# A vision tower layer on one core: how x is loaded and summed, which engine splits the stacks, where the mask is added, and in which order each engine works

## The chip, the cores and the metric

The kernel runs on one core of one Trainium2 chip. The metric is the device time of one execution in microseconds, as the median of several runs. Engines: TensorE (PE; its weight loads are PEld), VectorE (DVE), ScalarE (ACT), GpSimd (POOL), SyncE (SP, which here only issues DMAs).

## The reference, cut to what matters

```python
# x: (64, 12, 224, 224) f32
pooled = x.reshape(64, 12, 14, 16, 14, 16).sum(axis=(3, 5))        # sums of 16x16 patches
h = einsum('bcij,ce->bije', pooled, channel_weights)               # (64, 196, 192)
n = layernorm(h)
# attention of 12 heads with causal mask (-10000 above the diagonal), and
selection = softmax((n @ sel_w + sel_b) / temperature)[..., 1:]
_, idx = top_k(selection[..., 0], 14)          # 14 of 196 tokens of an image
h = h + (n with attn_output * selection added at the rows idx)
out = h + gelu(layernorm(h) @ in_weight.T + in_bias) @ out_weight  # hidden 768
```

Each token of h is a combination of 12 channel sums, so most of the work is done on 12 or 13 numbers for each token. Attention is computed for the 14 chosen tokens of each image alone.

## The kernel before, in words

The 64 images are 16 groups (g) of 4. For a group:

- **L, the patch sums.** x of a group comes in 7 tiles of 128 partitions x 2688 numbers (3 x 4 image rows of 224). `load_x` (L300) puts the first two of each four rows into a ring of 7 buffers, from SyncE's queue; when they have landed, GpSimd issues an accumulating DMA for the other two rows (`add_halves`, L339). `sum_tile` (L855) then reduces 1344 numbers to 42 on VectorE. After the seventh tile SyncE stores R to a scratch tensor (L307), waits for it and loads it back in another layout (Praw, L315). GpSimd adds the four quarters (L348 to L355).
- **A, the tokens.** `tm` (L444) multiplies by the moments; VectorE computes variance and the first reciprocal root (`var`), `zt` transposes z, `fm` copies it to FM. `log`, `e`, `sel` give the selection, `sl`, `top`, `st`, `slots` the 14 chosen tokens (MAX8 and MATCH_REPLACE8, L936 to L954, then one-hot Sg).
- **K, the stacks.** VectorE computes the second reciprocal root (`var2`), v26, and two differences; ScalarE splits them into bf16 parts (H, M, L, L642); TensorE transposes (L472) and ScalarE copies to Stk1 and Stk2 (L648, L653).
- **f and O, the dense FFN.** 12 matmuls `f` (L555) into one PSUM bank, each followed by a Gelu on ScalarE (L692) before the next may start. 7 output tiles `O` of 6 f32 matmuls (two passes each: 12 instructions, L567) and one bf16 (L571). Tile i takes the tokens i, i + 7, i + 14, ..., so its stationary operand is read with a step of 7 numbers (`tile_of`).
- **G and S, attention of the chosen tokens.** `ga`, `u` (L483 to L496), `sc` the scores (L506), the mask added and the maximum taken on VectorE (L1008, L1012), exponentials on ScalarE (L665), scaled by the reciprocal sum (L670), transposed (`et`, L512), copied (`t`, L674), `g` (L518), `at` (L527).
- **C, the FFN of the chosen tokens**, for two groups together: `xh` (VectorE, L1036 to L1044), `xt`, `fa`, `fb` (L542), `f2` (L547), `os` (L1051), and an indirect store from GpSimd (L362).

Every engine runs a `plan` by itself, a list of `stage:step:lag`; in period k it does the step for group k - lag. What comes first in the list is done first, and waits hold up all that is behind them. TensorE's and VectorE's lists before:

```
PE:  A:tm:1 S:sc:2 O:3:2 A:zt:1 O:4:2 O:5:2 S:et:2 K:tr1:1 S:g:2 K:tr2:1 f:0:1 o:6.0:2 f:1:1 ... f:6:1 o:6.6:2 A:sl:1
     f:7:1 at:0:2 ... f:11:1 O:0:1 A:st:1 O:1:1 G:ga:1 C:xt:2 C:fa:2 G:u:1 O:2:1 C:fb:2 C:f2:2
DVE: L:0 A:var:1 S:sc:2 A:log:1 L:1 A:var2:1 K:v:1 S:ri:2 L:2 K:d1:1 A:sel:1 L:3 K:d2:1 S:g:2 A:top:1
     L:4 S:at:2 A:slots:1 C:xh:2 L:5 G:ga:1 L:6 G:u:1 C:os:2
```

Before the periods, the weights are folded; the copies of these results from PSUM are VectorE's (`weights_heads`, `weights_attention`, `weights_ffn`, in `prepare`), between the first sums.

Of the kernel before, what the change touches and what calls it, by code (L numbers as in the profile page):

```python
# [6 lines left out]
N = IMG // PATCH  # L7
# [3 lines left out]
GB = 4  # L11
# [20 lines left out]
ODD = 64  # L32
PROWS = ODD + SLOTS
# [11 lines left out]
NX = 7  # L45
AHEAD = 2
END = NG + 3
# [60 lines left out]
def program(nc, x, cw, wqkv, bqkv, selw, selb, ow, ob, temp, w1t, b1, w2, consts, e48, e13r, out):  # L108
# [9 lines left out]
    with ExitStack() as ctx:  # L118
# [11 lines left out]
        def kc(name, rows=128):  # L130
# [20 lines left out]
        X = sb("X", [128, NX, TQ * QB // 2])  # L151
# [4 lines left out]
        FM = [sb(f"FM{i}", [ZR, T]) for i in range(2)]  # L156
        prod = sb("prod", [HALF, 2, BC])

        sc = {n: sb(n, [HALF, 2 * GB]) for n in ("var", "lr", "L", "t1", "t2", "s2", "al", "den", "rden")}
# [7 lines left out]
        Sg = sb("Sg", [HALF, 2, 2, SLOTS])  # L167
# [8 lines left out]
        RM = sb("RM", [ROWS, T])  # L176
        UB = sb("UB", [ZR, HP, 2, SLOTS])
# [28 lines left out]
        w_cw, w_ffn, w_att = sem("channel_weights_loaded"), sem("ffn_weights_loaded"), sem("attention_weights_loaded")  # L206
        x_in = [sem(f"x_loaded{k}") for k in range(NX)]
        x_added = [sem(f"x_halves_added{k}") for k in range(NX)]
# [23 lines left out]
        dve_S = Steps(sem("dve_attention"), "sm mx nm ri g0 g1 h1")  # L232
# [13 lines left out]
        dve_W = Steps(sem("dve_weights"), "wr0 ws0 xh0 h10 as0 ini idb ms ms2 wcs rf mr mr2 wcr bw0 bw1 wt ws cf cf2 raw sd sd2 s1 tp tz tmm tmd tmb m1 "  # L246
                      + " ".join(f"{n}{t}" for t in "MR" for n in splits.split()) + " q k v a4 b2 ob")
# [44 lines left out]

        def tile_of(ap, i):

            return ap.rearrange("p (m i) -> p i m", i=FT)[:, i, :]

        @block.sync
        def _(sp):
            def load_x(i, c):
                sp.dma_start(buffer_of(c), half_rows(i, c, 0)).then_inc(x_in[c % NX], 16)  # L300

            def after_tile(i, c):

                if c % XT == XT - 1:
                    g, r = 4 * i + c // XT, (c // XT) % 2
                    sp.wait_ge(dve_L, 4 * XT * i + c + 1)
                    sp.dma_start(scratch[bass.ds(g, 1)].rearrange("o p q -> (o p) q"), R[:, r, :]).then_inc(sums_out[r], 16)  # L307
                if not isinstance(i, int) or c + NX < NT:
                    sp.wait_ge(dve_L, 4 * XT * i + c + 1)
                    load_x(i, c + NX)  # L310
                if c % XT == XT - 1:
                    sp.wait_ge(sums_out[r], landed(g, r))
                    if exists(g - 2):
                        sp.wait_ge(pool_P.sem, pool_P.at(g - 2, "q23"))
                    sp.dma_start(Praw[:, r, :], sums_in[bass.ds(g, 1)].rearrange("o p q -> (o p) q")).then_inc(sums_back[r], 16)  # L315

            for c in range(NX):
                load_x(0, c)
            for c in range(AHEAD):
                after_tile(0, c)  # L320

            def body(i, k):
                for s in range(XT):
                    c = XT * k + s + AHEAD
                    if not isinstance(i, int) or c < NT:
                        after_tile(i, c)

            periods(nc.sync, body, 3, 2)
            for r in range(2):
                sp.wait_ge(sums_out[r], landed(NG - 2 + r, r))  # L330
                sp.wait_ge(y_out[r], landed(NG - 2 + r, r))
                sp.wait_ge(scat[r], landed(NG - 2 + r, r))

        @block.gpsimd
        def _(pool):
            def add_halves(i, c):
                pool.wait_ge(x_in[c % NX], use_of(i, c))
                by_itself(pool)
                pool.dma_start(buffer_of(c), half_rows(i, c, 1), accum_op=ALU.add).then_inc(x_added[c % NX], 16)  # L339
# [17 lines left out]
            def store_chosen(g, k, e, q):  # L357
# [4 lines left out]
                pool.indirect_dma_start(orows, bass.IndirectOffsetOnAxis(ap=idx[k % 4][:, 0:1], axis=0), OS[e][:, :], None  # L362
                                        ).then_inc(scat[e], 16)

            def body(i, k):
                for s in range(XT):
                    c = XT * k + s + AHEAD
                    if not isinstance(i, int) or c < NT:
                        add_halves(i, c)
                    if s == 1 and k % 2 == 0:  # L370
                        for e in range(2):
                            g = 4 * i + k - 4 + e
                            if active(g):
                                store_chosen(g, k + e, e, 2 * i + k // 2 - 2)
# [757 lines left out]
```

## Time and profile before

| | us |
|---|---|
| median of 3 runs (range) | 1082.65 (1079.1 to 1088.77) |
| the profiled execution | 1094.46 |
| its span, first to last instruction | 1092.3 |

The profile is of one execution. Its span is cut into engine busy times, waits and a chain of work that ended last. "Granted clock" is the share of full speed (2.4 GHz) that TensorE was given; it has the levels 1.2 and 2.4 GHz, and a mean between them is a mixture in time. A matmul's mean duration contains its latency; how densely a run of them follows is told by the timeline, which merges them.

### The profile page before, as it was taken

The numbers are of one execution on the slowest core, as the hardware profiler recorded it, in microseconds if no ns is written. First come the engines' busy times: TensorE is split into PE (matmuls) and PEld (weight loads), VectorE is DVE, ScalarE is ACT, GpSimd is POOL, SyncE is SP. The second block draws the span as 40 slices with busy tenths as digits, with TensorE's granted clock in tenths as the row PEclk, the third lists the DMA queues.
The fourth block names the chain that finished last, engine by engine and source line by source line (L and its number), as shares of the span: only waits on it lengthen the run. The fifth ranks groups of instructions, "written<-read, shape, count | busy, mean of one in ns | idle before, by whom it ended". The sixth has DMA issues, their size and how long they took to land.

```text
span 1092.3 us, 12505 instructions
## 1 busy us (share of the span) xinstructions
PE 797.3 (73%) x3860; PEld 624.2 (57%) x3860; DVE 489.6 (45%) x1468; ACT 349.2 (32%) x826; POOL 188.4 (17%) x180
## 2 busy tenths in 40 slices
PE   0632868686868868686877868686887969787885
PEld 0420747466565746466564846466573847567564
DVE  2653545446362535446272544546263454534111
ACT  0003152524333151524334151523325152424331
POOL 2130303013030403013030303013030222000000
PEclk9955669688887869688777879788676877788876
DMA  9999696958595687948595686958595594410000
GB/s 288 265 218 238 145 220 158 229 127 187 144 233 146 148 185 174 213 122 190 139 228 152 147 192 166 222 127 182 141 218 134 141 227 106 80 34 4 23 1 25
DMA packets 97864, 172.52 MB, mean 158 GB/s; under 512 B 5224, under 2 KB 94504, under 8 KB 97802
## 3 DMA queue, kind: packets, MB, share of 16 engines
q0 software_dynamic: 45312, 77.77, 40.4%
q1 hardware_dynamic: 48128, 81.90, 23.4%
q10 hardware_dynamic: 4362, 12.07, 3.4%
q8 instruction: 34, 0.56, 0.2%
q14 instruction: 28, 0.23, 0.1%
HBM read 158.99 MB, written 12.73 MB: 157 GB/s over the span
## 4 chain that ended last, share of the span: by engine, by line
PE 42%; DVE 19%; issue 13%; DMA 12%; ACT 12%; POOL 1%; ACTq 0%; POOLq 0%; DVEq 0%; SPq 0%
PE psO L567 13%; DMA X<-in_x 10%; PE psS L518 6%; PE psF L555 5%; ACT act L692 4%; DVE R L855 3%; PE psC L542 3%; PE psS L512 3%; ACT Sm L670 3%; PE psA L472 2%; PE psS L491 2%; PE psC L547 2%; ACT L692 2%; PE psS L527 2%; DVE mx L1012 2%
## 5 line engine op out<-in xcount | busy, mean ns | idle before, releaser
L567 PE MATMUL psO<-W,act 128*112 128x192 f32 x1344 | 362.8, 421 | 9.4 <-ACT act L692 9.4
L567 PEld LDWEIGHTS psO<-W,act 128*112 128x112 f32 x1344 | 319.3, 299 | 29.5 <-ACT act L692 13.5
L855 DVE TENSOR_REDUCE R<-X 128x42 f32<-128x1344 f32 x112 | 172.4, 1540 | 76.6 <-DMA X<-in_x 76.3
L339 POOL DMA_DIRECT2D X<-in_x x112 | 146.8, 2214 | 75.4 <-DMA X<-in_x 68.7
L692 ACT ACTIVATE act<-psF 128x392 f32<-128x392 f32 x192 | 95.4, 497 | 94.9 <-PE psF L555 94.7
L699 ACT ACTIVATE obuf<-psO 112x192 f32<-112x192 f32 x112 | 36.4, 325 | 276.9 <-PE psO L571 276.8
L555 PE MATMUL psF<-Stk,M1S 104*128 104x392 bf16 x192 | 79.6, 415 | 56.2 <-ACT act L692 55.6
L348 POOL TENSOR_TENSOR Pt<-Praw 48x196 f32<-48x196 f32 x16 | 8.6, 538 | 623.0 <-DMA Praw<-patch_sums 623.0
L512 PE MATMUL psS<-K,Sm 112*98 112x112 f32 x192 | 37.9, 383 | 74.4 <-ACT Sm L670 74.4
L555 PEld LDWEIGHTS psF<-Stk,M1S 104*128 104x128 bf16 x192 | 19.6, 102 | 120.4 <-ACT act L692 120.4
L1022 DVE TENSOR_TENSOR G<-psS,K 64x336 f32<-64x336 f32 x32 | 16.0, 500 | 142.6 <-PE psS L518 142.1
L512 PEld LDWEIGHTS psS<-K,Sm 112*98 112x98 f32 x192 | 32.2, 193 | 77.0 <-ACT Sm L670 77.0
L518 PE MATMUL psS<-ET,F 98*64 98x336 f32 x128 | 73.9, 758 | 1.5 <-ACT ET L674 1.5
L936 DVE MAX8 m8a<-psA 4x8 f32<-4x196 f32 x16 | 5.7, 358 | 140.6 <-PE psA L455 140.6
L472 PE MATMUL psA<-identb,SP 98*104 98x98 bf16 x256 | 27.3, 275 | 45.9 <-ACT SP L642 45.0
L472 PEld LDWEIGHTS psA<-identb,SP 98*104 98x104 bf16 x256 | 22.4, 184 | 65.2 <-issue 41.9
L362 POOL DMA_INDIRECT out<-OS,idx x16 | 15.4, 960 | 200.4 <-DVE OS L1051 197.9
L518 PEld LDWEIGHTS psS<-ET,F 98*64 98x64 f32 x128 | 26.7, 224 | 34.9 <-issue 31.7
L665 ACT ACTIVATE Sm<-Sm,nm 112x196 f32<-112x196 f32 x96 | 42.7, 446 | 8.4 <-DVE nm L1014 8.4
L542 PE MATMUL psC<-XH,W1T 97*128 97x112 f32 x192 | 37.7, 372 | 4.2 <-ACT XH L680 3.5
L527 PE MATMUL psS<-B,G 128*56 128x192 f32 x192 | 40.7, 337 | 0.0
L542 PEld LDWEIGHTS psC<-XH,W1T 97*128 97x128 f32 x192 | 34.9, 278 | 6.7 <-ACT XH L680 5.6
(190 smaller groups left out, 961.3 us busy)
## 6 DMA issues: line engine op xcount, KB each, us to landing
X<-in_x SPq DMA_DIRECT2D x112, 672.0 KB, 10.2
X<-in_x POOLq DMA_DIRECT2D x112, 672.0 KB, 16.5
out<-obuf ACTq DMA_DIRECT2D x16, 588.0 KB, 3.6
patch_sums<-R SPq DMA_DIRECT2D x16, 147.0 KB, 2.6
Praw<-patch_sums SPq DMA_DIRECT2D x16, 147.0 KB, 3.3
W1T<-in_w1t ACTq DMA_DIRECT2D x1, 576.0 KB
W<-in_w ACTq DMA_DIRECT2D x1, 576.0 KB
K<-in_consts ACTq DMA_DIRECT2D x1, 452.5 KB
```

What stands on the lines that cost most here:

```text
L339: pool.dma_start(buffer_of(c), half_rows(i, c, 1), accum_op=ALU.add).then_inc(x_added[c % NX], 16)
L472: mm = pe.transpose(to[0:SK, c0:c0 + HALF], SP[:, 2 * n + k, :, :].rearrange("p n c -> p (n c)"), identb[0:HALF, 0:HALF])
L512: mm = pe.transpose(psS[0:HALF, n // 4, (n % 4) * ROWS:(n % 4 + 1) * ROWS], Sm[:, j, k * HALF:(k + 1) * HALF], kc("ident")[0:ROWS, 0:ROWS])
L518: mm = pe.matmul(psS[0:ZR, 1 + i, 0:3 * ROWS], F[r][:, k, 0:ZR], ET[:, k * HP + 3 * i:k * HP + 3 * i + 3, :].rearrange("p j s -> p (j s)") ...
L527: mm = pe.matmul(psS[0:SLOTS, 0, 0:D], G2[:, j, :], B2[:, j, :], start=(j == 0), stop=(j == HP - 1))
L542: mm = pe.matmul(psC[:, (h % HA) * ROWS:(h % HA + 1) * ROWS], W1T[bias_first(k), k, h * 128:(h + 1) * 128], XH[bias_first(k), k, :], start ...
L555: pe.matmul(psF[:, 0:GT // 2], M1S[:, (n // 2) * 128:(n // 2 + 1) * 128], Stk1[u % 2][:, (n % 2) * (GT // 2):(n % 2 + 1) * (GT // 2)], sta ...
L567: pe.matmul(to, tile_of(act_sb[u % 2][:, m, :], i), W2[:, m, :], start=(m == 0), stop=False)
L665: act.activation(Sm[:, j, :], Sm[:, j, :], ACT.Exp, bias=nm[:, j:j + 1], accum_out=rsum[:, j:j + 1]).then_inc(act_S.sem, 1)
L692: act.activation(act_sb[u % 2][:, n // 2, (n % 2) * (GT // 2):(n % 2 + 1) * (GT // 2)], psF[:, 0:GT // 2], ACT.Gelu).then_inc(act_F1.sem, 1)
L699: act.activation(obuf[u % 2][:, i, :], psO[(i + u) % 2][0:OT, 0:D], ACT.Copy).then_inc(act_F2.sem, 1)
L855: dve.tensor_reduce(R[:, r, t * TQ * N:(t + 1) * TQ * N].rearrange("p (q j) -> p q j", q=TQ), v[:, :, :, :, :], AX.XY, ALU.add).then_inc(d ...
```

## The change

It does the following:

- x comes by plain loads of whole tiles, one buffer for each of the 7 tiles; no accumulating DMA is left (`ADDED` is empty). Tiles 1, 2, 4 and 6 are summed whole by VectorE (2688 numbers); for tiles 0, 3 and 5 GpSimd first adds the second half of the rows to the first (`halve`), and VectorE sums 1344.
- The second reciprocal root, v26 and both differences move from VectorE to GpSimd.
- Stk1 and Stk2 are written in tile order, by a strided read of PSUM, so that the stationary operands of O are contiguous.
- R's store and reload are issued by ScalarE (`R:st`, `R:ld`); SyncE only loads x.
- The mask is 56 more rows of the score matmul's operands (FM's rows 64 to 119 hold 0 or 1, UB's hold -10000 on a diagonal); the instruction that added it is gone, and the exponentials read PSUM.
- ScalarE takes the copies of the folded weights; the large weight loads wait for tiles 1, 3 and 6 of x. The first group's start is written out by hand.
- All four lists are new, O goes in three pieces, and VectorE and GpSimd count their periods one and two later.

```diff
-NX = 7
-AHEAD = 2
-END = NG + 3
+ADDED = ()
+HALVED = (0, 3, 5)
+END = NG + 5
-        X = sb("X", [128, NX, TQ * QB // 2])
+        X = [sb(f"X{k}", [128, TQ * QB // (2 if k in ADDED else 1)]) for k in range(XT)]
...
             def body(i, k):                                     # sync
+                g = 4 * i + k - 1
+                for t in range(XT):
+                    if active(g + 1):
+                        if exists(g):
+                            sp.wait_ge(dve_L, XT * g + t + 1)
...
+                            sp.dma_start(X[t][:, :], tile_in(g + 1, t).rearrange("o p q -> (o p) q")).then_inc(x_in[t], 16)
...
+            def halve(g, t):                                    # gpsimd
+                pool.wait_ge(x_in[t], loaded(g))
+                v = X[t][:, :].rearrange("p (q r w) -> p q r w", q=TQ, r=QR)
+                pool.tensor_tensor(v[:, :, 0:2, :], v[:, :, 0:2, :], v[:, :, 2:4, :], ALU.add).then_inc(x_halved[t], 1)
...
+            def second_variance(g):
+                pool.wait_ge(dve_R1.sem, dve_R1.at(g, "y2"))
...
+                rsqrt(g, pool_R2, n2)
...
+                    pool.tensor_tensor(d1[:, :, :], v26[:, :, :], SP[:, :, 0, :], ALU.subtract).then_inc(pool_K.sem, 1)
...
+            plan = ("H:3:1 P:s:2 H:5:1 c:s:5 A:var2:2 K:v:2 K:d1:2 K:d2:2 H:0:0").split()
...
-                    pe.matmul(to, tile_of(act_sb[u % 2][:, m, :], i), W2[:, m, :], start=(m == 0), stop=False)
+                    pe.matmul(to, act_sb[u % 2][:, m, i * OT:(i + 1) * OT], W2[:, m, :], start=(m == 0), stop=False)
...
+            plan = ("o:1.2:2 o:2.0:2 o:2.1:2 S:et:2 o:2.2:2 o:3.0:2 o:3.1:2 o:3.2:2 S:g:2 K:tr1:1 o:4.0:2 o:4.1:2 "
+                    "K:tr2:1 f:0:1 at:0:2 A:sl:1 at:1:2 at:2:2 f:1:1 o:4.2:2 f:2:1 o:5.0:2 f:3:1 A:st:1 o:5.1:2 "
+                    "f:4:1 G:ga:1 f:5:1 o:5.2:2 f:6:1 G:u:1 f:7:1 o:6.0:2 C:xt:2 o:6.1:2 C:fa:2 f:8:1 o:6.2:2 f:9:1 "
+                    "S:sc:1 f:10:1 C:fb:2 f:11:1 A:tm:0 C:f2:2 o:0.0:1 o:0.1:1 o:0.2:1 o:1.0:1 A:zt:0 o:1.1:1").split()
...
-                    act.activation(Stk1[u % 2][:, :], psA[:, :].bitcast(bf16)[0:SK, 0:GT], ACT.Copy).then_inc(act_K.sem, 1)
+                    act.activation(by_tile(Stk1[u % 2]), tokens_by_tile(psA[:, :].bitcast(bf16)[0:SK, 0:GT]), ACT.Copy).then_inc(act_K.sem, 1)
...
-                    act.activation(Sm[:, j, :], Sm[:, j, :], ACT.Exp, bias=nm[:, j:j + 1],
+                    act.activation(Sm[:, j, :], psS[0:ROWS, j // 2, (j % 2) * T:(j % 2 + 1) * T], ACT.Exp, bias=nm[:, j:j + 1],
...
+            plan = ("S:e2:2 S:e3:2 S:e4:2 S:e5:2 O:0:2 S:n:2 A:fm:1 O:1:2 A:e:1 S:t:2 K:H:1 K:M:1 O:2:2 K:L:1 O:3:2 "
+                    "R:st:0 K:k1:1 K:k2:1 f:0:1 f:1:1 f:2:1 f:3:1 f:4:1 R:ld:0 f:5:1 O:4:2 f:6:1 f:7:1 C:XH:2 O:5:2 "
+                    "G:rs:1 f:8:1 C:ga:2 O:6:2 f:9:1 f:10:1 C:gb:2 f:11:1 S:e0:1 S:e1:1").split()
...
-                    dve.tensor_tensor(Sm[:, :, :].rearrange("p (k j) t -> p k j t", k=3),
-                                      psS[0:ROWS, :, 0:2 * T].rearrange("p k (j t) -> p k j t", j=2),
-                                      RM[:, :].unsqueeze(1).unsqueeze(1).broadcast_to([ROWS, 3, 2, T]), ALU.add).then_inc(dve_S.sem, 1)
...
+            plan = ("A:sel:2 S:g:3 L:0:0 A:top:2 S:at:3 A:slots:2 G:ga:2 C:xh:3 L:1:0 G:u:2 L:2:0 S:sc:2 A:var:1 "
+                    "L:3:0 S:ri:2 A:log:1 L:4:0 C:os:3 L:5:0 L:6:0").split()
```

## Rows read from the trace of the kernel before

**Rows 1.** The profile page: the span and its instructions

```profile
span 1092.3 us, 12505 instructions
```

**Rows 2.** Two windows: length, busy us by engine, granted clock, DMA share, GB/s

```profile
0.00:60.00 60.00, 18.28 (x164) 14.13 (x164) 29.06 (x70) 1.28 (x1) 11.96 (x13) 1.00 1.05 275
503.30:626.30 123.00, 95.73 (x456) 75.15 (x456) 58.13 (x176) 43.41 (x103) 23.31 (x24) 0.79 0.74 172
```

**Rows 3.** One line's instructions, f: ns min/median/max, first and last start

```profile
L555 PE MATMUL psF<-Stk,M1S x192: 331/340/527, 100.5 to 1029.3; 104*128 104x392 bf16 x192
```

**Rows 4.** The chain that ended last, in order of time, 540 to 630 us

```profile
539.23 2.55 DMA patch_sums<-R
...
547.37 8.21 DMA X<-in_x
```

**Rows 5.** Waits, whole run: total us, times, longest us

```profile
DVE R L855 <- DMA X<-in_x: 76.3, 19, 17.3
```

**Rows 6.** Timeline: start, us, twelve f32 matmul instructions of 192 columns

```profile
555.85 4.20 PE L567 MATMUL psO<-W,act 128*112 128x192 f32 x12
...
618.22 2.21 PE L547 MATMUL psC<-W,actS 128*120 128x192 f32 x12 [0.45 <-ACT actS L686]
...
622.89 2.75 PE L567 MATMUL psO<-W,act 128*112 128x192 f32 x12
```

**Rows 7.** Weight loads by line: ns min/median/max, first and last start

```profile
L567 PEld LDWEIGHTS psO<-W,act x1344: 275/300/311, 115.5 to 1067.3; 128*112 128x112 f32 x192
...
L506 PEld LDWEIGHTS psS<-FM,UB x192: 169/173/308, 132.1 to 1045.0; 64*112 64x112 f32 x192
```

**Rows 8.** Groups of VectorE: busy us, mean ns of one

```profile
L855 DVE TENSOR_REDUCE R<-X 128x42 f32<-128x1344 f32 x112 | 172.4, 1540 | 76.6 <-DMA X<-in_x 76.3
...
L1008 DVE TENSOR_TENSOR Sm<-psS,RM 112x1176 f32<-112x1176 f32 x16 | 22.0, 1377 | 5.8 <-PE psS L506 5.8
```

**Rows 9.** GpSimd's elementwise work: a group, and one memset with its ns

```profile
L348 POOL TENSOR_TENSOR Pt<-Praw 48x196 f32<-48x196 f32 x16 | 8.6, 538 | 623.0 <-DMA Praw<-patch_sums 623.0
...
L1127 POOL MEMSET const-float32-0.0<- x1: 99/99/99, 0.4 to 0.4; 128x1 f32 x1
```

**Rows 10.** SyncE's DMA queue: packets, MB, share of 16 engines over the span

```profile
q1 hardware_dynamic: 48128, 81.90, 23.4%
```

**Rows 11.** Timeline, choosing tokens: first and last of eight VectorE instructions

```profile
534.26 0.36 DVE L936 MAX8 m8a<-psA 4x8 f32<-4x196 f32 x1 [8.81 <-PE psA L455]
...
537.26 0.35 DVE L954 TENSOR_TENSOR srow<-cum,mask 4x196 f32<-4x196 f32 x1
```

**Rows 12.** Timeline, queries and scores: ga, UB's two copies, and a score block

```profile
545.41 0.52 PE L483 MATMUL psS<-Sg,F 98*112 98x56 f32 x4
...
548.47 0.90 DVE L1001 TENSOR_TENSOR UB<-psS,K 64x336 f32<-64x336 f32 x2
...
620.81 2.16 PE L506 MATMUL psS<-FM,UB 64*112 64x196 f32 x12
```

**Rows 13.** Timeline, softmax at the end of the run: table load to ET's copies

```profile
1048.69 1.28 ACT L665 ACT_TABLE_LOAD   x1
...
1058.35 1.41 ACT L674 ACTIVATE ET<-psS 98x448 f32<-98x448 f32 x3 [2.35 <-PE psS L512]
```

**Rows 14.** Groups of ScalarE in the stacks: busy us, mean ns of one

```profile
L653 ACT ACTIVATE Stk<-psA 104x784 bf16<-104x784 bf16 x16 | 13.2, 823 | 67.1 <-PE psA L472 67.1
...
L642 ACT ACTIVATE SP<-v 98x624 bf16<-98x624 f32 x16 | 11.7, 730 | 27.4 <-DVE v L975 27.4
```

**Rows 15.** Timeline, chosen tokens normalised: first and last VectorE instruction of xh

```profile
600.57 0.35 DVE L1036 BATCH_NORM_STATS2 bst<-h 120x6 f32<-120x192 f32 x1
...
604.43 0.38 DVE L1044 TENSOR_SCALAR xh<-h,mv,y_lnC 120x192 f32<-120x192 f32 x1
```

**Rows 16.** Timeline, first variance: F's copy, and its last product

```profile
557.07 0.37 DVE L895 COPY F<-psA 98x216 f32<-98x216 f32 x1
...
560.61 0.26 DVE L904 TENSOR_TENSOR F<-F,y_ln 98x96 f32<-98x96 f32 x1
```

More of the change, by code:

```diff
@@ L32 @@
 ODD = 64
+KM = ZR + SLOTS
 PROWS = ODD + SLOTS
@@ L317, in _ @@
[L317 to L320, printed above, removed]
-            def body(i, k):
[L323 to L328, printed above, removed]
+            def body(i, k):
+                g = 4 * i + k - 1
[3 more added lines that the diff above has]
+                            sp.wait_ge(dve_L, XT * g + t + 1)
+                        if t in ADDED:
+                            sp.dma_start(half_tile(t), half_rows(g + 1, t, 0)).then_inc(x_in[t], 16)
+                        else:
+                            sp.dma_start(X[t][:, :], tile_in(g + 1, t).rearrange("o p q -> (o p) q")).then_inc(x_in[t], 16)
@@ L329, in _ @@
+            periods(nc.sync, body, 3, 3)
             for r in range(2):
@@ new lines, in _ @@
+            plan = ("H:3:1 P:s:2 H:5:1 c:s:5 A:var2:2 K:v:2 K:d1:2 K:d2:2 H:0:0").split()
+            def body(i, k):
+                for what in plan:
+                    stage, step, lag = what.split(":")
+                    g, u = 4 * i + k - int(lag), (k - int(lag)) % 4
+                    if not active(g):
+                        continue
+                    if stage == "X":
+                        add_halves(g, int(step))
+                    elif stage == "H":
+                        halve(g, int(step))
+                    elif stage == "P":
+                        sum_quarters(g, u % 2)
+                    elif stage == "K":
+                        stage_K(g, u, step)
+                    elif stage == "A":
+                        second_variance(g)
+                    elif u % 2:
+                        for e in range(2):
+                            store_chosen(g - 1 + e, u - 1 + e, e, pair_of(i, k, lag))
@@ L383, in _ @@
+            periods(nc.gpsimd, body, 5, 2)
         @block.tensor
@@ L712, in body @@
                     g, u = 4 * i + k - int(lag), (k - int(lag)) % 4
-                    if not active(g):
+                    if not active(g) or (stage == "R" and isinstance(g, int) and g == 0):
                         continue
                     if stage == "C":
-                        if k % 2:
-                            step_C(2 * i + k // 2 - 1, step)
+                        if u % 2:
+                            step_C(pair_of(i, k, lag), step)
                     elif stage == "O":
@@ L722, in body @@
                     else:
[L723 removed]
+                        {"A": step_A, "G": step_G, "K": step_K, "R": step_R, "S": step_S}[stage](g, u, step)
             weights()
[L726 removed]
+            weights_heads()
+            step_R(0, 0, "st")
+            step_R(0, 0, "ld")
+            weights_attention()
+            periods(nc.scalar, body, 6, 2)
         @block.vector
```

418 lines of the change are left out of this document (219 added, 199 removed).

## The prediction

> **What bounds the kernel now.** Read first the page's span [rows 1] and the windows [rows 2]. Two groups (one without and one with the FFN of the chosen tokens, C) take 123.0 us, or 61.5 each. No engine fills that: TensorE is busy 95.73 us of it at a mean granted clock of 0.79, VectorE 58.13, ScalarE 43.41, GpSimd 23.31, and DMA 0.74. So it is a ring of steps that hand over to each other, while the in-order lists leave each engine idle at its own hand-over. The first matmul f starts at 100.5 us and the last at 1029.3 [rows 3]; that is 928.8 us for 15 periods and one set of twelve f's, and 63.0 us of the span lie behind it.
>
> Second, the chain in order of time [rows 4]: from the store of the sums at 539.23 to GpSimd's next x DMA at 547.37 are 8.1 us, for store, reload and three quarter sums; then 8.21 us of waiting for x. GpSimd issues the accumulating half of x behind the quarter sums, SyncE issues loads behind the store. VectorE's wait for x totals 76.3 us [rows 5]. Third, the timeline: twelve matmul instructions of 192 columns take 2.75 us for an O tile, 2.21 us for `f2`, and 4.20 us for an O tile when the clock is low [rows 6]. At the high clock O is thus held back by something `f2` does not have, its stationary operand with a step of 7: such a load is 300 ns in the median, a contiguous one of the same 112 columns 173 [rows 7].
>
> **Part by part, for one group.**
>
> *O in tile order.* Seven tiles at 2.75 - 2.21 = 0.54 us less are 3.8 us, and the bf16 loads a little more: 4.2. At the low clock the columns themselves bind (4.20 us is more than either), and nothing is gained. Bounds 0 to 4.6; I take 4.2, as TensorE will seldom be idle for long. The price is a strided read by ScalarE's two stack copies, 0.82 us each [rows 14]. No strided read of PSUM is timed there; I bound it from nothing to as much again, 1.6 us a group, and take 0.5.
>
> *Sums.* VectorE's 1344 numbers take 1.54 us [rows 8]. The mask's addition, 1176 numbers with the same kind of fixed part, takes 1.38, so a number costs about 1 ns and a whole tile 1.54 + 1.40 = 2.94. Four whole and three halved tiles are 16.4 us against 10.8: 5.6 more. VectorE loses the mask's 1.38 and the moved root, v26 and differences, some 25 small instructions, about 4.2 us together (an estimate at 0.17 us each). It stays at 29 us of a group [rows 2], below any period in question, but its 3-us pieces now stand in the ring.
>
> *GpSimd.* 196 numbers take 0.538 us and a memset of one number 0.099 [rows 9]; the difference gives 2.24 ns a number, hence 3.1 us for `halve` (1344), from 1.5 (if it ran as VectorE) to 3.7 (if all scaled): 9.3 us for three. The second root is 18 instructions of 8 numbers, one waiting for the other. Bounds 0.10 and 0.54 us each plus a hand-over near 0.1; I take 0.25, the row nearest in size being the memset: 4.5 us. v26 is 0.8 and a difference 0.56. All with the quarter sums 18 us a group, against 61.5 available.
>
> The Trainium skill's GPSIMD Engine Reference, section Elementwise, gives 4497 ns for a tensor_tensor of 2048 numbers, in proportion 2.95 us for `halve`: 0.5 us a group less, which changes nothing here.
>
> *x.* Plain loads moved 81.90 MB in 23.4% of the span [rows 10], 255.6 us, thus 320 GB/s; 9.6 MB a group and 0.9 of output and sums are 33 us. Every buffer is refilled a period ahead. With no transfer behind GpSimd's list, the 8.21 us of [rows 4] are hidden by the period of lead; if a period fell to 33 us they would return. The store and reload sit in ScalarE's list before the stack copies and after the fourth Gelu. `R:st` waits for the last sum, and K:k1, both stack copies and all Gelus are queued behind it; I cost it at 0.4 us of issue and up to 1 us of wait.
>
> *The new ring, without C.* First from f to f: choosing the tokens is 537.61 - 534.26 = 3.35 us [rows 11], after an estimated 2.5 us of transposes and the sum L:0; then, estimated from like instructions, 0.6 for `st`, 1.0 for h1 and the one-hot. From ga to the end of UB's copies are 549.37 - 545.41 = 4.0 [rows 12], and the sum L:1 is put between them, 2.94. Scores 2.16, the last two f's 1.3. Total 17.9. Then from the last f to the next first: matmul 0.34 [rows 3] and Gelu, estimated from its size beside [rows 14], 0.50; from the table load to the end of ET's copies 1059.76 - 1048.69 = 11.1 [rows 13], plus 0.9 because L:3 (1.54) stands before `ri`; the stacks 2 x 0.73 + 0.57 and two differences, with hand-overs 3.5 [rows 9, 14]; two transposes and the first copy with `R:st` 2.5. Total 18.8. The other branch, tm 1.1 (an estimate: four small matmuls behind the last f), variance 3.8 [rows 16], root 4.5 and v26 0.8, arrives after 10.2, when the first part has used 11.9: covered, by 1.7 us and the transposes. Period 36.7. With C, the normalisation on VectorE is 604.81 - 600.57 = 4.2 [rows 15] and fb 1.1: 42.0. Mean 39.4. TensorE's own work is 95.73 x 0.79 / 2 = 37.8 us a group at the high clock [rows 2], less 4.2 for O: 34 us, now spread between these steps, so it has little slack: some of the steps at the low clock, hand-overs and collisions in the lists I estimate at 10%, 3.6 us. I take 43 us, with 39 and 50 as ends.
>
> *Start.* Group 0's x and the weights are 11.4 MB, at the 275 GB/s of the first 60 us [rows 2] 41.5 us; last sum 2.9; VectorE's weight splits and two sums of group 1, 13; variance 3.8; root and v26 5.5; stacks 3.5, transposes and copy 2. First f at 72 instead of 100.5; bounds 62 and 85. *End.* The old table load of the last scores stands at 1048.69, 19.4 us behind the last f [rows 3, 13]; in the new list it follows after 0.84, so 63.0 - 18.6 = 44.4; with the other steps 43. Twelve f's of the last group without sums between them 15.
>
> *Sum.* 72 + 15 x 43 + 15 + 43 = 775, and 2 us around the span (1094.46 against 1092.3) 777. The median stands at 1082.65 / 1094.46 = 0.989 of the profiled execution: **769 us**.
>
> **The rivals.**
>
> *GpSimd's small instructions are dear.* At 0.54 + 0.18 each the root takes 13 us, not 4.5, and the 1.7 us of cover are gone: with the transposes as only cover, 7 more a period. A period of 50: 72 + 750 + 58 + 2 = 882, times 0.989: 872. For it: [rows 9] have no dependent small instruction. Against: the memset.
>
> *GpSimd and VectorE block each other.* Where a `halve` holds up a VectorE instruction of the variance or the selection, it costs up to 3.1 us each; half of the three in the ring is 4.7 us a period, 47.7, and by the same sum 838 us. In [rows 16] the steps follow undisturbed, but there GpSimd does nothing of this kind.
>
> The Trainium skill's SBUF — State Buffer, section Who interferes with whom, says that a VectorE instruction with two SBUF inputs and a GpSimd instruction that reads SBUF exclude each other for the whole instruction. By that rule this rival is real; no row of before has the pair at the same time.
>
> *The clock stays at 0.79* [rows 2]. 34 us at the high level become 43 on TensorE alone, and with 4 of unhidden latency 47: 828 us.
>
> *Only the x waits and O go; the ring is not otherwise loosened.* 61.5 less 4.1, less 4.2: 53, and 917 us.
>
> *Slower.* The place is GpSimd's list: the differences d1, d2 and then `halve` 0, for which VectorE's L:0 waits, with the choosing of tokens and all of the next f's behind. This loop decides once a period is over 64 us: it has to grow by 21 us and the 1.7 of cover, so its 21 chained instructions would have to take 1.3 us each instead of 0.25. Then the time is 1095 or more (a period of 65). Against: [rows 9] end at 0.54.
>
> **How the numbers follow.** Forecast 0.58, dear small instructions 0.15, low clock 0.10, blocking 0.08, only x and O 0.07, slower 0.02. The likeliest case has its own range of 715 to 825 (periods of 40 to 46). To leave out no more than 2 in 10 it must take in most of the first rival: 705 to 880. A measurement of this kernel tells about 1% from no change. Faster by over 1%: 0.96, within 1% 0.01, slower 0.03.
>
> **What would show it.** O tiles of twelve instructions at 2.2 us; whole sums at 2.9 us and `halve` at 3.1; no wait for x over 1 us after the start; the first f near 72 us; granted clock over 0.85; GpSimd's root near 4.5 us and not named by ScalarE's H; VectorE busy some 70%. Wrong it would be if VectorE's waits name GpSimd, if `R:st` holds ScalarE for several us before the stack copies, or if whole windows of two groups last over 100 us.

## The result, and the profile after

| | before | after |
|---|---|---|
| median (range), us | 1085.71 (1079.1 to 1090.33) | **788.65** (780.08 to 795.12) |
| the profiled execution | 1094.46 | 791.8 |
| its span | 1092.3 | 790.0 |

The ratio is 0.7213, with a 95% interval of 0.7129 to 0.7298: 27.9% less time. Ratios, here and below, are worked out from the executions of the faster of two states alone (in after 780.08 and 785.50 us), medians from all executions; by the medians it is 297 us. The forecast was 769, with a range of 705 to 880.

The profile page of after, its span, busy times and the queue of x (MB, and share of 16 engines):

```profile
span 790.0 us, 12358 instructions
...
PE 609.0 (77%) x3860; PEld 494.3 (63%) x3860; DVE 599.0 (76%) x1092; ACT 345.4 (44%) x839; POOL 277.9 (35%) x484
...
q1 hardware_dynamic: 16128, 154.15, 51.8%
```

All of x now goes through SyncE's queue, at 154.15 MB in 51.8% of 790.0 us, or 377 GB/s. TensorE and VectorE are level, near 77%.

The windows view, one pair of groups (columns as in [rows 2]):

```profile
374.87:463.85 88.98, 73.99 (x458) 60.58 (x457) 74.47 (x129) 42.18 (x104) 34.59 (x60) 0.88 0.64 239
```

It is 88.98 us where it was 123.0 [rows 2]. TensorE's 95.73 us became 73.99, by the clock (0.79 to 0.88) and by O. But VectorE is busy 74.47 us, 37.2 a group, and the forecast had 29. The groups view by form says with what:

```profile
L968 DVE TENSOR_REDUCE R<-X 128x42 f32<-128x2688 f32 x64 | 188.2, 2940 | 0.1
L354 POOL TENSOR_TENSOR X<-X 128x1344 f32<-128x1344 f32 x48 | 144.8, 3029 | 45.1 <-DMA X<-in_x 45.1
...
L1015 DVE TENSOR_TENSOR den<-Ex 98x8 f32<-98x8 f32 x16 | 77.9, 4869 | 1.9 <-ACT Ex L744 1.9
L968 DVE TENSOR_REDUCE R<-X 128x42 f32<-128x1344 f32 x48 | 74.3, 1547 | 9.2 <-POOL X L354 8.5
...
L763 ACT ACTIVATE Stk<-psA 104x784 bf16<-104x784 bf16 x16 | 13.2, 823 | 18.3 <-PE psA L548 10.4 <-DVE R L968 7.9
```

Whole sums 2.94 us and `halve` 3.03, as worked out. VectorE waits for no x in the steady state, where it had waited 76.3 us [rows 5]. The strided stack copy is 823 ns, as the contiguous one was [rows 14]. One line is out of all proportion: `den`, the sum of two rows of 8 numbers in the selection (`A:sel`), takes 4.87 us in the mean. The timeline shows why:

```profile
389.60 0.73 ACT L757 ACTIVATE SP<-v 98x624 bf16<-98x624 f32 x1
...
392.36 6.00 POOL L354 TENSOR_TENSOR X<-X 128x1344 f32<-128x1344 f32 x2
...
392.85 5.53 DVE L1015 TENSOR_TENSOR den<-Ex 98x8 f32<-98x8 f32 x1
...
398.41 0.20 DVE L1017 RECIPROCAL rden<-den 98x8 f32<-98x8 f32 x1
398.65 0.17 DVE L1021 TENSOR_TENSOR TS<-Ex,rden 98x8 f32<-98x8 f32 x1
398.85 1.03 DVE L1093 TENSOR_TENSOR G<-psS,K 64x336 f32<-64x336 f32 x2
399.91 1.55 DVE L968 TENSOR_REDUCE R<-X 128x42 f32<-128x1344 f32 x1
...
399.93 1.53 PE L605 MATMUL psS<-B,G 128*56 128x192 f32 x4 [4.22 <-DVE G L1093]
```

GpSimd runs two `halve`s in a row, H:0 of one period and H:3 of the next, from 392.36 to 398.36. `den` begins at 392.85 and ends at 398.38, with them. Its input had been ready since 387.23, so it was not waiting for that. Its neighbour TS, of the same form, takes 0.17. The same happens in 13 of the 16 groups, and each time `den` ends with the second `halve`. Behind `den` stand G, the sum L:0 and the choosing of tokens; TensorE waits 4.22 us for G. So the theory to be tested is: **`den` is held up by `halve`, and that stands in the ring.** The view of waits lists this as PE's wait for VectorE's G, 54.2 us in all, and names GpSimd nowhere: a blocked instruction looks busy.

The source view of f, after:

```profile
L635 PE MATMUL psF<-Stk,M1S x192: 326/339/535, 94.4 to 755.8; 104*128 104x392 bf16 x192
```

By the sum of the prediction the period is (755.8 - 94.4 - 15) / 15 = 43.1 us; below, every "period" is worked out from this row in the same way.

### The profile page after: what moved, and what is told of

Read it like the earlier page. It is cut to its first block, busy times and chain, and to the rows that moved or that the text cites. A ratio compares the mean times of both kernels' runs of the same rounds, so it can differ in the third digit from the quotient of the medians.

```text
span 790.0 us, 12358 instructions
## 1 busy us (share of the span) xinstructions
PE 609.0 (77%) x3860; PEld 494.3 (63%) x3860; DVE 599.0 (76%) x1092; ACT 345.4 (44%) x839; POOL 277.9 (35%) x484
## 3 DMA queue, kind: packets, MB, share of 16 engines
q1 hardware_dynamic: 16128, 154.15, 51.8%
## 4 chain that ended last, share of the span: by engine, by line
PE 43%; DVE 41%; issue 8%; DMA 3%; ACT 3%; ACTq 1%; POOL 1%; DVEq 0%; POOLq 0%
DVE R L968 14%; PE psO L650 11%; DVE den L1015 10%; PE psS L605 7%; PE psS L582 5%; PE psF L635 5%; PE psC L620 4%; DVE a_lnC L978 3%; PE psS L567 2%; DMA WT<-in_e 2%; DMA X<-in_x 1%; DVE b_lnC L980 1%; DVE G L1093 1%; PE psA L535 1%; PE psS L594 1%
## 5 line engine op out<-in xcount | busy, mean ns | idle before, releaser
L968 DVE TENSOR_REDUCE R<-X 128x42 f32<-128x2688 f32 (+1 forms) x112 | 260.1, 2343 | 9.2 <-POOL X L354 8.5
L650 PE MATMUL psO<-W,act 128*112 128x192 f32 x1344 | 263.5, 338 | 3.7 <-issue 2.3
L650 PEld LDWEIGHTS psO<-W,act 128*112 128x112 f32 x1344 | 221.9, 183 | 9.8 <-issue 4.9
L354 POOL TENSOR_TENSOR X<-X 128x1344 f32<-128x1344 f32 x48 | 144.8, 3029 | 45.1 <-DMA X<-in_x 45.1
L605 PE MATMUL psS<-B,G 128*56 128x192 f32 x192 | 58.9, 468 | 54.2 <-DVE G L1093 54.2
L1015 DVE TENSOR_TENSOR den<-Ex 98x8 f32<-98x8 f32 x16 | 77.9, 4869 | 1.9 <-ACT Ex L744 1.9
L791 ACT ACTIVATE Sm<-psS,nm 112x196 f32<-112x196 f32 x96 | 39.2, 427 | 4.9 <-issue 4.7
L796 ACT ACTIVATE Sm<-Sm,rinv 112x196 f32<-112x196 f32 x96 | 35.2, 446 | 12.8 <-DVE rinv L1088 12.7
L594 PE MATMUL psS<-ET,F 98*64 98x336 f32 x128 | 39.6, 452 | 0.0
L582 PE MATMUL psS<-FM,UB 120*112 120x196 f32 x192 | 39.2, 359 | 0.0
L582 PEld LDWEIGHTS psS<-FM,UB 120*112 120x112 f32 x192 | 36.2, 200 | 0.8
```

What stands on the lines that cost most here:

```text
L354: pool.tensor_tensor(v[:, :, 0:2, :], v[:, :, 0:2, :], v[:, :, 2:4, :], ALU.add).then_inc(x_halved[t], 1)
L582: mm = pe.matmul(psS[0:ROWS, j // 2, (j % 2) * T:(j % 2 + 1) * T], UB[:, j, :, :].rearrange("p k s -> p (k s)"), FM[r][:, :], start=True, ...
L594: mm = pe.matmul(psS[0:ZR, 1 + i, 0:3 * ROWS], F[r][:, k, 0:ZR], ET[:, k * HP + 3 * i:k * HP + 3 * i + 3, :].rearrange("p j s -> p (j s)") ...
L605: mm = pe.matmul(psS[0:SLOTS, 0, 0:D], G2[:, j, :], B2[:, j, :], start=(j == 0), stop=(j == HP - 1))
L650: pe.matmul(to, act_sb[u % 2][:, m, i * OT:(i + 1) * OT], W2[:, m, :], start=(m == 0), stop=False)
L791: act.activation(Sm[:, j, :], psS[0:ROWS, j // 2, (j % 2) * T:(j % 2 + 1) * T], ACT.Exp, bias=nm[:, j:j + 1], accum_out=rsum[:, j:j + 1]). ...
```

## The experiments

All times are medians; "after" is the changed kernel. Experiments 1 to 4 ran one after the other on one chip, 5 to 8 on a second, 9 to 11 on a third and 12 on a fourth, each set beside the kernel before (medians of 1085.67 to 1089.84 us there). Differences below are those of the medians. By the ratios three of them come out otherwise: 93 us for 97.5 (experiment 1), 49 for 55 (experiment 2) and 20 for 13.5 (experiment 3); the others agree within 5 us.

**1. The selection moved forward.** In after's list of VectorE `A:sel` stands first, behind all seven sums. Here it stands behind L:4 of the period before.

```diff
-            plan = ("A:sel:2 S:g:3 L:0:0 A:top:2 ...
-                    "L:3:0 S:ri:2 A:log:1 L:4:0 C:os:3 L:5:0 L:6:0").split()
+            plan = ("S:g:3 L:0:0 A:top:2 ...
+                    "L:3:0 S:ri:2 A:log:1 L:4:0 A:sel:1 C:os:3 L:5:0 L:6:0").split()
```

> One edit: VectorE's step sel (den, rden, TS) is done four list places earlier, behind the sum L:4 of the period before, when GpSimd runs only small instructions. Theory 1 (blocking): den takes 4.87 us in the mean because two halves of x follow each other on GpSimd while it wants its second SBUF input; moved, it takes 0.17 us, the 4.7 us leave the ring and 15 periods give 70 us: about 715 us, between 705 and 735. Theory 2 (the ring is VectorE's amount of work, and the block only moves to the next two-input instruction): den is short, but another VectorE instruction grows by the same, and the time stays within 775 to 795.

Measured: **691.14** (685.46 to 699.59), ratio 0.6356 (0.6286 to 0.6425). Groups and source views:

```profile
L1015 DVE TENSOR_TENSOR den<-Ex 98x8 f32<-98x8 f32 x16 | 2.5, 156 | 2.5 <-ACT Ex L744 2.5
...
L635 PE MATMUL psF<-Stk,M1S x192: 326/339/534, 97.8 to 663.6; 104*128 104x392 bf16 x192
```

`den` is back at 156 ns and the period is 36.7. One entry of a list, moved, is worth 97.5 us. That is more than the 75 us that `den` lost in all (77.9 - 2.5), and more than was expected (705 to 735).

**2. No halves.** All seven tiles are summed whole, and GpSimd halves nothing; the selection stays late.

```diff
-HALVED = (0, 3, 5)
+HALVED = ()
-            plan = ("H:3:1 P:s:2 H:5:1 c:s:5 A:var2:2 K:v:2 K:d1:2 K:d2:2 H:0:0").split()
+            plan = ("P:s:2 c:s:5 A:var2:2 K:v:2 K:d1:2 K:d2:2").split()
```

> HALVED is empty: GpSimd halves nothing, VectorE sums all seven tiles whole, 3 x 1.39 = 4.2 us more of VectorE a group. Theory 1 (blocking): den (4.7 us a group) and the chosen tokens' root (3.4 us in two groups) lose their waits, 6.4 us a group, against 4.2 more of sums: 2.2 us a period less, about 755 us, 740 to 775. Theory 2 (VectorE's amount of work sets the ring): 15 x 4.2 = 63 us more, about 850 us.

Measured: **733.36** (727.55 to 738.32), ratio 0.6758 (0.6677 to 0.684); period 38.7. VectorE sums for 327.2 us instead of 262.5, 65 us more, and the kernel is 55 us faster, a little more than the blocking theory had expected (740 to 775). With this list the offloading that was to relieve VectorE costs more than it relieves.

**3. Stacks in token order**, as before: O's stationary operand has a step of 7 again, and the stack copies read PSUM contiguously. Late selection, three halves.

```diff
-                    act.activation(by_tile(Stk1[u % 2]), tokens_by_tile(psA[:, :].bitcast(bf16)[0:SK, 0:GT]), ACT.Copy)
+                    act.activation(Stk1[u % 2][:, :], psA[:, :].bitcast(bf16)[0:SK, 0:GT], ACT.Copy)
...
-                    pe.matmul(to, act_sb[u % 2][:, m, i * OT:(i + 1) * OT], W2[:, m, :], ...
+                    pe.matmul(to, tokens_by_tile(act_sb[u % 2][:, m, :])[:, i, :], W2[:, m, :], ...
```

> The stacks are copied in token order again and O's stationary operands are read with a step of 7, as before the change; all else is the new kernel. If TensorE's work is in the ring with little slack, as the prediction has it, an O tile is 0.6 us longer at the high clock and 16 groups give up to 67 us: 830 to 860 us. If VectorE sets the ring and TensorE has slack, 785 to 805 us. If the strided PSUM read of the new stack copies costs ScalarE something, its copies are now shorter than 0.82 us.

Measured: **802.19** (800.61 to 803.66), ratio 0.7395 (0.7324 to 0.7465). The weight load of O is 298 ns in the median and 177 in after, and O's matmuls are busy 325.6 us instead of 263.5; the time grew by 13.5 alone. TensorE had slack, because it waited for the selection in any case. The block had not gone, but moved in part onto TS, which takes 168 ns in after:

```profile
L1021 DVE TENSOR_TENSOR TS<-Ex,rden 98x8 f32<-98x8 f32 x16 | 46.4, 2903 | 1.0
...
L1015 DVE TENSOR_TENSOR den<-Ex 98x8 f32<-98x8 f32 x16 | 39.9, 2492 | 2.7 <-ACT Ex L744 2.7
```

In every second group `den` gets through before the two `halve`s and TS meets them; the two steps together lose as much as in after (86.3 us against 80.6).

**4. The accumulating DMA back**, for the three tiles that GpSimd halved.

```diff
-ADDED = ()
-HALVED = (0, 3, 5)
+ADDED = (0, 3, 5)
+HALVED = ()
-            plan = ("H:3:1 P:s:2 H:5:1 c:s:5 A:var2:2 K:v:2 K:d1:2 K:d2:2 H:0:0").split()
+            plan = ("X:3:1 P:s:2 X:5:1 c:s:5 A:var2:2 K:v:2 K:d1:2 K:d2:2 X:0:0").split()
```

> Tiles 0, 3 and 5 come as half tiles with an accumulating DMA from GpSimd, in the places of its three halves; the new lists stay. If the accumulating DMA itself held x back in the kernel before, waits of VectorE for x return and the time is 800 us or more. If its place behind the quarter sums was the trouble and the transfer is hidden in the new order, VectorE has the same sums as now but no blocking: den 0.17 us, about 715 to 740 us.

Measured: **851.44** (845.93 to 854.38), ratio 0.7861 (0.7783 to 0.7939). From the waits:

```profile
DVE R L968 <- DMA X<-in_x: 149.6, 17, 16.3
```

`den` is 246 ns here, and yet it is 118 us behind experiment 2, the one without halves: VectorE waits for x about once a group. In the group at 415 us GpSimd issues two of its transfers at 415.46, behind the differences; VectorE could go on at 417.29 and waits 8.85 us, to 426.14. Such a transfer takes 11.9 us in the median from issue to landing. How much of the wait is the late issue and how much the transfer itself was not separated. Plain loads are the largest single gain that I could isolate: 118 us beside experiment 2, and 63 beside after, which pays for its `halve`s.

**5. Early selection and token order** (1 and 3).

> The early sel of e1_sel_early (691 us), with the stacks in token order and O's stationary operands read with a step of 7. With tile order undone in the changed kernel the time grew by 14 us only, while VectorE was held up. Theory: TensorE had slack there and has little here (busy 83%), so a good part of 0.6 us x 112 tiles = 67 us comes out: 735 to 760 us. Rival: tile order is worth little in any case, 700 to 712 us.

Measured: **757.96** (754.61 to 760.69), ratio 0.6972 (0.6943 to 0.7001): 66.8 us over experiment 1. That is 16 x 4.2, as the theory had it (735 to 760). Tile order is worth 13.5 us (20 by the ratios) while VectorE holds TensorE up, and three to five times that when it doesn't.

**6. The store of the sums later**, with the early selection: `R:st` behind both stack copies in ScalarE's list.

```diff
-                    "R:st:0 K:k1:1 K:k2:1 f:0:1 ...
+                    "K:k1:1 K:k2:1 R:st:0 f:0:1 ...
```

> The early sel of e1_sel_early, and ScalarE issues R's store behind both stack copies instead of ahead of them. At the start K:k1 of group 0 waited 8.4 us for group 1's last sum behind that store. Theory: first f at 89 instead of 97.7 us and 5 to 9 us less in all, 682 to 687 us; in later periods nothing, since sums are done in time. Rival: the first f is earlier but the second group is bound by its own sums, so the time stays at 691 within 4.

Measured: **697.1** (687.86 to 703.02), ratio 0.6369 (0.6322 to 0.6416). The first f starts at 86.7 instead of 97.8, and the time is no better. In after and in experiment 1 ScalarE waits for the last sum once, in the first group, 7.9 and 8.4 us. Moved, the wait stands before the first Gelu, 4.8 us, and f, which waits for Gelu, stands still with it (TensorE's longest such wait is 6.0 us). Of a start 11 us earlier nothing arrives at the end; the last f starts at 667.0, 3.4 us later than in experiment 1.

**7. GpSimd's H:5 moved forward**, with the early selection, so that no `halve` stands beside the root of the chosen tokens' normalisation.

```diff
-            plan = ("H:3:1 P:s:2 H:5:1 c:s:5 ...
+            plan = ("H:3:1 H:5:1 P:s:2 c:s:5 ...
```

> The early sel of e1_sel_early, and GpSimd halves tile 5 ahead of the quarter sums instead of behind them, so that no half runs beside the chosen tokens' root. Blocking theory: y_lnC's mean falls from 462 to about 175 ns and xh's from 850 to about 400 ns, 10 us in 8 pairs: 680 us, 676 to 686. Rival: the halves now stand in a row of three and hold up another two-input instruction of VectorE (the scan, srow) or the quarter sums: 690 us or more.

Measured: **760.84** (757.25 to 764.17), ratio 0.6995 (0.6961 to 0.7029): 70 us slower than experiment 1. A group and the timeline:

```profile
L1040 DVE TENSOR_SCALAR mask<-sl 4x196 f32<-4x196 f32 x16 | 31.6, 1972 | 0.5
```

```profile
380.21 9.00 POOL L354 TENSOR_TENSOR X<-X 128x1344 f32<-128x1344 f32 x3
...
387.00 2.32 DVE L1040 TENSOR_SCALAR mask<-sl 4x196 f32<-4x196 f32 x1
```

The normalisation is free (its instructions 187 to 268 ns), but three `halve`s in a row now reach to 389.21, and the mask of the chosen tokens, 0.25 us in after, ends at 389.32. It has one SBUF input. TensorE waits for its result (srow), 29.6 us in all. The blocking was not removed but moved to a dearer place: the rival held. The wait of 29.6 us does not make up the 70; TensorE is also busy 635.3 us against 575.9 in experiment 1 for the same matmuls, at a mean granted clock of 0.860 against 0.936.

**8. The mask added by VectorE again**, with the early selection: an instruction like that of [rows 8] (112x1176, 1379 ns), the 56 rows of the score matmul taken out.

```diff
+                    dve.tensor_tensor(Sm[...], psS[0:ROWS, :, 0:2 * T], RM[:, :]..., ALU.add)
-                    dve.tensor_reduce(mx[...], psS[0:ROWS, :, 0:2 * T]..., AX.X, ALU.max)
+                    dve.tensor_reduce(mx[:, :], Sm[:, :, :], AX.X, ALU.max)
```

> The early sel of e1_sel_early, with the mask added on VectorE again (one instruction of 1.38 us a group from PSUM, the maximum and the exponentials read SBUF) and the score matmuls without the 56 mask rows. If that step is in the ring: 15 x 1.4 = 21 us more, 712 us, 705 to 720. If TensorE's tiles cover it: 691 within 5.

Measured: **718.98** (710.8 to 723.93), ratio 0.6593 (0.6551 to 0.6634): 27.8 us over experiment 1, or 1.74 a group for an instruction of 1.38. It stands in the ring whole (25.7 us by the ratios, 1.6 a group).

**9 to 11.** Number 9 has the early selection and no halves (1 and 2). Number 10 has the early selection and halves tiles 0 and 3 alone. Number 11 is after with tiles 3 and 5 alone halved: no two `halve`s in a row at `den`, and the selection late. The entries `H` of the other tiles leave GpSimd's list with them (not shown).

```diff
 (9)
-HALVED = (0, 3, 5)
+HALVED = ()
 (10)
-HALVED = (0, 3, 5)
+HALVED = (0, 3)
 (11)
-HALVED = (0, 3, 5)
+HALVED = (3, 5)
```

> The first experiment (sel early) and the second (all sums whole, GpSimd halves nothing) together: no instruction of VectorE can be held up by GpSimd's halves any more. VectorE sums 3 x 1.4 = 4.2 us more a group than with sel early alone. Theory A (with sel early the halves hold up almost nothing, so what they save is in the ring): 691 + 16 x 4.2 = 758 at most, less 16 x 1.2 for the chosen tokens' normalisation that is no longer held up: 720 to 745. Rival (what the halves save is lost again in blocking, or the sums lie in VectorE's slack): 685 to 700.

> Sel early, with tile 5 summed whole: GpSimd halves tiles 0 and 3 alone, and no halve is left beside the normalisation of the chosen tokens (its instructions were 350 and 270 ns where they are 190 elsewhere, some 3.4 us a pair of groups). VectorE sums 1.4 us more a group. Theory A (the sum stands in the ring, and so does the normalisation in every second group): plus 16 x (1.4 - 1.7) = -5: 686, 680 to 700. Rival (only the sum counts, since L:5 stands late in the list beside f's and the normalisation has slack): 691 + 22 = 713.

> The changed kernel with one edit: tile 0 is summed whole, so GpSimd halves tiles 3 and 5 alone and does not do two in a row where den stands; the order of VectorE's and all other lists is that of the changed kernel (sel still late). Theory (den is lost because it falls into two halves in a row, 5 us a group): with a single halve, which starts before den and ends before or shortly after it, den takes 0.2 to 3 us; VectorE sums 1.4 us more a group: 789 + 22 - 16 x (3 to 5) = 731 to 763. Rival (the place of sel in the list is what costs, by the wait for the selection's turn behind the last sums, and den's length is only waiting that would stand elsewhere): 789 + 22 = 811, at least 785.

Measured: 9 **725.07** (720.88 to 728.29), ratio 0.669 (0.6647 to 0.6734); 10 **699.72** (699.05 to 700.55), ratio 0.6445 (0.6405 to 0.6485); 11 **780.08** (758.29 to 782.59), for which there is no interval.

Number 9 closes a square of four:

| | three halves | no halves |
|---|---|---|
| selection late | 788.65 | 733.36 |
| selection early | 691.14 | 725.07 |

Without halves the place of the selection is worth 8 us, which the intervals do not tell from nothing; with them, 97.5. So of the 97.5 some 89 (86 by the ratios) come from GpSimd's halves standing beside it, and at most 8 from the order itself. And the halves, which cost 55 us with the late selection, save 34 with the early one.

Number 10 lies at the upper edge of what was expected (680 to 700). The third `halve` saves 8.6 us, though the intervals of numbers 1 and 10 overlap: 22.4 us of sums (283.1 against 260.7 on L968) stand against the normalisation that it blocks (27.4 against 18.0 us on its root and xh). Number 11's row of `den`:

```profile
L1015 DVE TENSOR_TENSOR den<-Ex 98x8 f32<-98x8 f32 x16 | 36.3, 2268 | 1.9 <-ACT Ex L744 1.9
```

`den` is still held up, by one `halve` (2.27 us) and not by two (4.87): the mechanism shows without any step being moved, and with the length expected (0.2 to 3 us). The time does not settle it. Three executions took 779.14 to 782.59 us, one 758.29, and after took 780.08 to 795.12. So the gain may be near nothing, or some 25 us; by 2.6 us less of `den` and 1.4 more of sum it would be 1.2 x 15 = 18. Whether the 731 to 763 expected were met stays open.

The profile is of the execution of 779.14, and only that one is spoken of here. Its span is 45 us above that of experiment 2 (777.3 against 732.1), where VectorE's own busy time is only 10 us longer (572.8 against 562.7). TensorE is busy 620.9 us against 590.5 for the same 3860 matmuls. First a stretch of number 11 in the windows view, then its block of 24 query matmuls in the timeline:

```profile
400.30:409.00 8.70, 5.90 (x36) 4.19 (x36) 7.54 (x17) 3.97 (x6) 0.00 (x0) 1.00 0.86 324
409.00:416.00 7.00, 7.00 (x46) 5.72 (x45) 5.15 (x10) 1.80 (x5) 3.40 (x4) 0.59 0.32 86
416.00:424.00 8.00, 7.41 (x33) 6.44 (x31) 3.75 (x2) 2.97 (x8) 3.16 (x3) 0.72 0.90 324
```

```profile
411.81 2.81 PE L567 MATMUL psS<-ZY,A 64*64 64x56 f32 x24
```

and the same block in experiment 2, the kernel without halves:

```profile
461.50 1.60 PE L567 MATMUL psS<-ZY,A 64*64 64x56 f32 x24
```

TensorE idles a third of the stretch behind `den` (400.30 to 409.00), and is then granted 0.59 and 0.72 of full speed, a mixture of its two levels, for 15 us. A block that takes 1.60 us at 2.4 GHz takes 2.81. In experiment 2 TensorE is busy 7.92 of the 8.70 us of the same stretch (452.00 to 460.70), and the clock stays at 1.00 behind it. The block takes 2.81 us in number 7 too, behind the wait for the mask (at 395.26). So a blocked instruction of VectorE seems to be paid for twice: once as a wait, once as a lower clock behind it. The mean granted clock of the profiled executions fits this: 0.887 after, 0.878 in number 11, 0.860 in number 7, 0.921 in number 2, 0.936 in number 1 and 0.948 in number 9. But it is lowest in number 4 (0.829), where VectorE waits for x: any wait that holds TensorE up may do it.

**12. The store later, with two halves** (10 and 6). ScalarE waits 34.5 us in 14 groups for the last sum in number 10.

```diff
-                    "R:st:0 K:k1:1 K:k2:1 f:0:1 ...
+                    "K:k1:1 K:k2:1 R:st:0 f:0:1 ...
```

> The tenth experiment (sel early, GpSimd halves tiles 0 and 3) with the store of the sums (R:st) put behind the two stack copies in ScalarE's list. In the tenth ScalarE waits 34.5 us in 14 groups for the last sum before the first stack copy; in the first (with three halves) it was 8.4. Theory (that wait stands in the ring, between the last f and the next first f): 15 x 2.0 = 30 us less at most, of which TensorE's own work covers a part: 675 to 692, and it would be the fastest version. Rival (TensorE or VectorE bounds the group by then, so the wait only moves, to Gelu or to the tokens): 695 to 702. The store leaves at most 2 us later, and its landing has time until the quarter sums of the next period.

Measured: **708.62** (702.29 to 714.88), ratio 0.6486 (0.645 to 0.6523), 8.9 us slower than number 10: neither expected value held. The intervals touch, so what is clear is only that nothing was gained. The waits:

```profile
PEld psF L635 <- ACT act L820: 45.9, 55, 7.9
DVE mx L1082 <- PE psS L582: 39.1, 15, 5.3
PE psF L635 <- ACT act L820: 28.6, 25, 7.5
...
ACT act L820 <- DMA patch_sums<-R: 19.6, 10, 2.9
```

The reload (`R:ld`) stands in ScalarE's list behind the fifth Gelu and waits for the store to land; a later store makes it wait in ten groups, between two Gelus, where TensorE waits with it (28.6 us, 9.5 in number 10). In the original place the wait for the sum seems to lie beside O; this was not tested.

## Why the prediction was right, and where it was not

**The total** was 20 us low (769 against 788.65), well inside the range. It holds larger errors of both signs: 22.4 us too few at the start, 8.8 too many at the end. Two slips of the working did no harm. By [rows 8] a number costs (1540 - 1377) / 168 = 0.97 ns, so a whole tile would be 2.84 us, and the 2.94 that was written, and measured, is luck; and `R:ld` stands behind the fifth Gelu, not the fourth.

**The period of 43** was met, 43.1, but not for the stated reason: that it came out is luck. The ring was worked out at 39.4 plus 10% for low clock and collisions. Freed of the block at `den`, it is 36.7 (experiment 1), so the ring itself was over-estimated by 2.7 and the 3.6 us of allowance weren't needed. The 6.4 us between are, all but some 0.5 of the order itself (experiments 2 and 9), what GpSimd's halves cost there: 4.7 of `den` in the mean of all groups, some 0.7 more at the root of the chosen tokens (its lines and xh: 38.4 us in all against 27.4), and, by what is left, the clock.

**The rival "GpSimd and VectorE block each other"** had 0.08. Its mechanism is the one in this kernel, and its price, 4.7 us a period, was right to a tenth for `den`. This agreement is luck too: the price was half of three `halve`s, each holding up one instruction, and measured was one instruction that two in a row hold up, in 13 of 16 groups. I had it as an addition to a ring of 43; it came on top of a shorter one. The step that failed is the weighing: [rows 16] could not speak against it, since GpSimd does nothing of the kind in before, and that should have left the chance open rather than low. I should also have laid the two lists beside each other: H:0 and H:3 are neighbours across the period's end, and the first entry of VectorE's list faces them.

Beside the rows: the Trainium skill's SBUF — State Buffer, section Who interferes with whom, lets a `tensor_reduce` never contend on this chip, a two-input VectorE instruction contend with GpSimd's reads, and a `tensor_scalar` in a two-port mode too. The rows agree: the whole sums stay at 2940 ns beside `halve`, `den` does not, nor does number 7's mask, and G, which reads PSUM and one SBUF operand, runs undisturbed: 1.03 us for two in experiment 1, at 385.90, beside two `halve`s from 385.02 to 391.04. The section also says that whoever issues first gets the ports for the whole of its instruction. `den` shows more: it stood ready during the first `halve` and still let the second pass.

**"VectorE stays at 29 us."** 37.2 in after. The windows view of experiment 1, two periods:

```profile
374.00:448.00 74.00, 64.35 (x438) 53.01 (x437) 55.91 (x118) 38.72 (x96) 32.81 (x59) 0.95 0.70 266
```

Without the block it is 55.91 / 2 = 28.0 us a group: the instructions had been added up correctly, and what was missing was the time in which one of them stands still.

**O in tile order, -4.2 us a group.** Tiles of twelve take 2.13 us in the timeline of after (2.2 forecast). In after only 13.5 us of it are in the time (experiment 3; 20 by the ratios), in the freed kernel 67 (experiment 5), which is 4.2 x 16. So the size is right, and "TensorE will seldom be idle for long" was wrong for after. The copies' strided read costs nothing (823 ns), where I had 0.5 us a group.

**The mask** was worth its duration: 1.74 us a group (experiment 8).

**GpSimd's root:** 18 instructions of 0.20 to 0.24 us from 382.88 to 388.62, 5.7 us instead of 4.5. The cover of 1.7 us is used up in this group: ScalarE's H starts at 389.60, with v ready at 389.56, and is not named as waiting. The rival of 0.54 us each is refuted.

**x:** hidden in the steady state, as forecast; experiment 4 shows what plain loads are worth, 118 us.

**Start, 72 us (62 to 85): wrong, 94.4.** The timeline of after:

```profile
51.27 0.39 ACTq L774 DMA_DIRECT2D patch_sums<-R  x1
...
62.46 0.33 ACTq L779 DMA_DIRECT2D Praw<-patch_sums  x1
...
67.00 0.54 POOL L363 TENSOR_TENSOR Pt<-Praw 48x196 f32<-48x196 f32 x1 [11.49 <-DMA Praw<-patch_sums]
...
69.90 0.38 DVE L994 COPY F<-psA 98x216 f32<-98x216 f32 x1 [4.84 <-PE psA L520]
...
80.50 0.51 PE L526 MATMUL psA<-K,F 98*64 98x98 f32 x2 [1.44 <-ACT B L738]
```

The sum of the start had no term for the store and the reload: 15.7 us from 51.27 to 67.00, while the loads of group 1 are under way. VectorE's weight splits and two sums run beside it until 65.05, so 4.8 us of it are left as a wait (at 69.90). Another 4.9 us lie before it: the last sum of group 0 ends at 49.26, where 44.4 had been worked out. The largest term comes last: the first stack copy waits 7.9 us for group 1's last sum, which stands in `R:st`. At most 1 us had been forecast for that; it is true in the steady state of after, but not in numbers 10 and 9 (34 and 40 us in all), where VectorE sums more. `zt` too waits for the folded weights, whose copies ScalarE now makes (80.50), but that is off the path: v is ready at 81.46 and H starts at 81.49. **End, 43 us:** 34.2, so the 22.4 us too few at the start were paid back in part, by 8.8. The scale of 0.989 also failed; after's median is 0.996 of its profiled execution, 5 us.

**Clock** over 0.85: 0.887.

**What is open.** How much of the 89 us is wait and how much clock was not separated: no experiment holds the clock. The 297 us were taken apart only for x, tile order, the mask and the `halve`s; the root on GpSimd, the store and reload on ScalarE, the copies of the folded weights and the new lists were not undone one by one. The fastest version is experiment 1 (691.14, 12.4% below after), which the intervals do not tell from numbers 6 and 10. Its remaining blocks at the root of the chosen tokens (y 462 ns, xh 850 in the mean) went only for another block (number 7) or for longer sums (number 10).

## What to carry to other kernels

When work is given to GpSimd, lay its list beside VectorE's and keep every VectorE instruction with two SBUF operands, or a copy or `tensor_scalar` with a single one, away from GpSimd's long instructions, most of all where two of these follow each other; in this kernel the sums (`tensor_reduce`) and G, which reads PSUM, could stand beside them. A tiny instruction with a mean of microseconds in the groups view is the sign of it, since the waits name no one. An edit's worth depends on what else is in the ring: tile order gave 13.5 to 20 us behind the block and 67 without it, and halving on GpSimd cost 55 us with one list and saved 34 with another.

## What was not expected of the hardware

- A VectorE instruction of 98x8 numbers that met two GpSimd instructions of 3.0 us in a row was held up until both were done (5.53 us, a mean of 4.87 over 16), and not let in between them.
- A VectorE instruction with one SBUF input (`tensor_scalar`, 4x196) was held up as well, 1.97 us in the mean against 0.25; so was a copy of 64x192 in the preparation of after, 3.12 us beside a `halve` and 0.25 without one in experiment 1.
- ScalarE's read of PSUM with a step of 7 bf16 numbers costs no more than a contiguous one, 823 and 824 ns, while TensorE's weight load with a step of 7 costs 298 ns against 177.
- The small store of the sums, while x's loads were under way, took 11.2 us until the reload could be issued (51.27 to 62.46), and 7.9 us in the median of 16, where such a store took 2.55 before [rows 4]. Why it takes longer was not isolated.
